# Two of the nine moves of an attention round issued by ScalarE instead of SyncE

## The reference

```
latent_kv = x @ w_kv_down ; kv = latent_kv @ w_kv_up ; k, v = split(kv)
q = x @ w_q
att = softmax(where(causal, q @ k.T * 64**-0.5, -inf))
y = (att @ v) @ w_out
```

## Time and profile before

| | |
|---|---|
| median of 3 runs | 1727.76 us (1726.07 to 1730.22) |
| the profiled execution | 1725.72 us, of which its span 1724.4 us |
| PE busy | 1661.7 us, 96% of the span |
| DVE busy | 1228.0 us, 71% |
| ACT busy | 848.3 us, 49% |
| POOL busy | 867.3 us, 50% |
| moves issued by SP | 864 (576 from prob, 288 from hx) |
| granted clock of PE | 0.997 of full speed |

### The profile page before, as it was taken

How to read it: one execution, slowest core, us unless ns; L and a number is a source line. 1 busy time by engine, 2 the same in 40 slices (tenths; PEclk the granted TensorE clock), 3 DMA queues, 4 the chain that set the end, 5 groups by cost and what they waited for, 6 DMA issues and landing times.

```text
span 1724.4 us, 41078 instructions
## 1 busy us (share of the span) xinstructions
PE 1661.7 (96%) x16518; PEld 1135.8 (66%) x16518; DVE 1228.0 (71%) x2678; ACT 848.3 (49%) x1864; POOL 867.3 (50%) x1123
## 2 busy tenths in 40 slices
PE   8999999999999999999999999999999999999997
PEld 5566685768566667566856667756684666766667
DVE  4988947727698994762679887675367999677445
ACT  5667624233576763422357765432245776433233
POOL 2788852231188884232128888314114888741410
PEclk9999999999999999999999999999999999999999
DMA  6566572231565655041346655405035666620504
GB/s 191 125 150 153 137 183 85 42 58 47 159 148 137 146 141 168 1 73 26 83 138 154 146 138 137 149 2 98 1 113 137 143 150 142 156 104 2 98 0 124
DMA packets 143853, 189.11 MB, mean 110 GB/s; under 512 B 34512, under 2 KB 107696, under 8 KB 142640
## 3 DMA queue, kind: packets, MB, share of 16 engines
q1 hardware_dynamic: 125472, 179.14, 42.4%
q10 hardware_dynamic: 18192, 7.35, 1.9%
HBM read 88.32 MB, written 13.16 MB: 59 GB/s over the span
## 4 chain that ended last, share of the span: by engine, by line
PE 66%; DVE 14%; ACT 5%; SPq 4%; POOL 4%; DMA 3%; issue 3%; ACTq 0%; POOLq 0%; DVEq 0%
PE scores L470 13%; PE bank L681 9%; PE scores L661 8%; PE bank L470 5%; DVE prob L800 4%; SPq L1011 4%; ACT prob L916 3%; DMA placed<-prob 3%; POOL placed L864 3%; PE scores L1718 2%; PE bank L718 2%; PE bank L708 2%; PE scores L441 2%; PE scores L1780 2%; PE bank L712 2%
## 5 line engine op out<-in xcount | busy, mean ns | idle before, releaser
L864 POOL COPY placed<-prob 32x768 f32<-32x768 f32 x448 | 368.3, 822 | 213.9 <-DVE prob L800 183.1
L301 POOL TENSOR_TENSOR rstd<-rstd,minus_half 128x2 f32<-128x2 f32 x96 | 69.9, 729 | 502.1 <-DVE rstd L300 500.0
L681 PEld LDWEIGHTS bank<-placed,v_t 128*64 128x64 f32 x4608 | 250.7, 137 | 75.7 <-issue 74.1
L681 PE MATMUL bank<-placed,v_t 128*64 128x128 f32 x4608 | 272.6, 274 | 11.8 <-DMA placed<-prob 9.0
L661 PE MATMUL scores<-k_t,q_t 64*128 64x512 f32 (+3 forms) x1536 | 274.0, 496 | 1.2 <-DVE neg_max L793 1.2
L800 DVE STREAM_TRANSPOSE prob<-prob 128x1536 f32<-128x1536 f32 x128 | 222.6, 1764 | 44.9 <-ACT prob L916 44.6
L793 DVE CUSTOM_DVE_ANT_0 mod_rows<-scores,hx 128x128 f32<-128x128 f32 (+7 forms) x256 | 190.7, 745 | 32.3 <-PE scores L661 32.3
L661 PEld LDWEIGHTS scores<-k_t,q_t 64*128 64x128 f32 x1536 | 130.1, 187 | 113.1 <-issue 92.2
L864 POOL COPY placed<-hx 32x768 f32<-32x768 f32 x224 | 184.3, 823 | 34.5 <-DVE hx L800 17.9
L916 ACT ACTIVATE prob<-mod_rows,neg_max 128x128 f32<-128x128 f32 (+2 forms) x192 | 137.7, 717 | 117.3 <-DVE neg_max L793 113.6
L793 DVE CUSTOM_DVE_ANT_0 x<-scores,hx 128x128 f32<-128x128 f32 (+7 forms) x256 | 192.7, 753 | 0.0
(11 more groups left out here) (256 smaller groups left out, 3139.0 us busy)
## 6 DMA issues: line engine op xcount, KB each, us to landing
placed<-prob SPq DMA_DIRECT2D x576, 96.0 KB, 2.5
f<-in_L_ffn_f SPq DMA_DIRECT2D x16, 2048.0 KB, 13.4
placed<-hx SPq DMA_DIRECT2D x288, 96.0 KB, 2.2
inverse_wide<-inverse_scratch SPq DMA_DIRECT2D x64, 256.0 KB, 4.2
slots_scratch<-high_rows SPq DMA_DIRECT2D x16, 512.0 KB, 6.3
inter<-slots_scratch SPq DMA_DIRECT2D x32, 256.0 KB, 4.8
mod_rows<-mod_scratch SPq DMA_DIRECT2D x32, 128.0 KB, 5.1
out<-x SPq DMA_DIRECT2D x16, 256.0 KB, 2.1
```

What stands on the lines that cost most here:

```text
L301: step = pool.do(lambda e, ts=ts: nc.gpsimd.tensor_tensor(rstd[:, ts], rstd[:, ts], minus_half[:, ts], op=ALU.pow), var, filled)
L681: last = nc.tensor.matmul(out_bank[rows_, at_:at_ + P], v_t[pair % 2][:, j, rows_], placed[m % 2][:, :, head, first_block(m, i) + j, :], s ...
L864: nc.gpsimd.tensor_copy(placed[m % 2][target * GROUP:(target + 1) * GROUP, source, :, :, :], prob[m % 3][source * GROUP:(source + 1) * GRO ...
```

## The change

The nine moves of a round are split. SP issues the first seven. The other two, (source 1, target 2) and (source 3, target 2), are issued by ACT, in a new function `last_moves`, behind the two exponentials of the first tile of the next round; in a round of type 0 this is in front of `store_inverse` (and, in round 3, of a projection's copy). The two of the stage's last round are issued behind ACT's last exponentials. Semaphores and counts stay the same: PE waits for all nine.

```diff
+        SP_MOVES, ACT_MOVES = MOVES[:7], MOVES[7:]
...
+            def last_moves(m):
+                e.wait_ge(flow["shuffled"], base["shuffled"] + HEADS * (m + 1))
+                if m > 1:
+                    e.wait_ge(flow["values_done"], base["values_done"] + m - 1)
+                for source, target in ACT_MOVES:
+                    e.dma_start(placed[m % 2][target * GROUP:(target + 1) * GROUP, source, :, :, :],
+                                prob[m % 3][source * GROUP:(source + 1) * GROUP, target, :, :, :]
+                                ).then_inc(flow[MOVED[m % 2]], 16)
...
                 for i in range(large):
                     for head in range(HEADS):
                         exponential(m, i, head)
+                    if i == 0 and m > 0:
+                        last_moves(m - 1)
                     if i == 0 and first_of_pair and m > 0:
                         if m == 3:
                             job(*jobs[0])
...
                 if first_of_pair:
                     next_weights(m)
+            last_moves(ROUNDS - 1)
             store_inverse(PAIRS - 1)
...
-                for source, target in MOVES:
+                for source, target in SP_MOVES:
```

## The result

| | before | changed |
|---|---|---|
| median | 1726.97 us (4 runs) | 1749.85 us (4 runs, 1745.74 to 1752.51) |
| ratio | | 1.0129, 95% interval 1.011 to 1.0148 |
| span of the profiled execution | 1724.4 us | 1746.9 us |

The change made the kernel slower by 1.3%, about 22 us. The sign and one of two mechanisms were forecast; the size is 1.7 times the forecast 13 us, at the very edge of the likeliest case's own range (1732 to 1750 us) and inside the full one.

What follows compares the result with a forecast made beforehand. PE, 96% busy, was taken as the bound; ACT's issues would make the DVE and ACT loop slower: 3 x 3.3 + 4.3 = 14.2 us, taken as 13, forecast 1741 us. Range 1726 to 1757, likeliest case 1732 to 1750.

Steps and rivals of the forecast that it cites:

- The gain on SP's side: SP's seven issues instead of nine: last move starts 1.27 us earlier; gain between nothing and PE's 10.6 us of waits.
- The price of an issue: One move issued on ACT: taken as 0.55 us, bounds 0.39 and 0.59 us; two with gaps 1.18 us.
- A: Rival: an ACT issue costs 0.39 us, PE sets the pace, the landing gain wins; 1719 us, chance 0.12.
- B: Rival: small issue price but landings don't move, or more slack in the loop; about 1728 us, chance 0.21.
- D: Rival: ACT and SP sequencers take turns issuing, two moves cost 2.3 us; about 1830 us, chance 0.03.
- Type 0, 1.15 us: Type 0 rounds: the moves in front of `store_inverse` delay ACT's next exponential from 576.46 to 577.6, cost 1.15 us.
- path M: Type 0's late transpose, SP's issues, last landing, PE's values; forecast for an isolated round: last move still 0.6 us earlier.
- The loop and its sum: DVE and ACT loop, per triple (a pair's three rounds): 22.98 + 1.35 = 24.33 us against PE's floor of 23.85.
- The check on the first triple: A stage's first triple, 22.98 us, taken to confirm the 23.0 us loop, so 0.87 us to spare.
- Cost 0.2 us: Type 2 rounds: issues end at 570.59, the large exponential started at 570.36; cost 0.2 us in the loop.
- rival C: ACT pays more than 0.59 us an issue, say 0.75; a triple takes 25.1 us; 1764 us, chance 0.10.
- The end of the stage: Behind round 21 POOL works without pause and PE waits for it, so the stage's lateness passes on one to one.

Runs made afterwards that it cites:

- both places mended: Changed kernel, ACT's two issues moved behind the third tile's exponentials in type 0 and behind the second large exponential in type 2: 1723.7 us, ratio 0.9975.
- only type 2 mended: Changed kernel, ACT's two issues moved behind the second large exponential in type 2, left behind the first tile in type 0: 1739.0 us, ratio 1.0064.
- type 0 alone: Changed kernel, but ACT issues moves in rounds of type 0 only; SP keeps all nine for the others: 1740.0 us, ratio 1.008.
- the one that only kept the engine busy for the same 1.2 us: Kernel before, no DMA moved, thirteen extra 128x1 exponentials on ACT behind the first tile's in type 0: 1737.5 us, ratio 1.0049.
- types 1 and 2: Changed kernel, but SP keeps all nine moves that fall in rounds of type 0: 1740.4 us, ratio 1.0077.
- type 2 alone: Changed kernel, but ACT issues moves in rounds of type 2 only: 1742.5 us, ratio 1.0081.
- type 2's place alone left bad: Changed kernel, ACT's issues put behind all tiles but the largest (type 0: third tile); types 1 and 2 unchanged: 1739.7 us, ratio 1.0074.

## Why the prediction was right, and where its size was off

- **The gain on SP's side.** Forecast: between nothing and 10.6 us. PE's waits for placed fell to 2.0 us, so the mechanism of the gain is real. In the change it is hidden by what follows; with both places mended (2.9 us of waits) the kernel is 0.25% faster, 4 of the 10.6 us.
- **The price of an issue.** Taken 0.55 us, measured 0.57 to 0.60 in the median. Rivals A, B and D of the prediction fall. The page "Perfetto Trace Analysis" of the Trainium skill (section "DMA Instruction — HWDGE (DVE, Sync)") has the wait for the shared descriptor generator inside the duration. A full turn of waiting isn't what this trace shows: beside SP's 0.59 us issues ACT's were no longer than that in the median.
- **Type 0, 1.15 us.** The third exponential is 1.3 us later against the first, since the second move costs 0.65 us and `store_inverse` 0.60 instead of 0.51. That this is a cost of its own is shown by the run with only type 2 mended (+11 us). The run with type 0 alone (+13 us) and the one that only kept the engine busy for the same 1.2 us (+9 us) show the cost of the delay too, but there SP still has nine moves, and it arrives through them (path M). The prediction had this path as an isolated round, "the last move still 0.6 us earlier"; in the change, with seven moves on SP, it was right not to count it.
- **The loop and its sum.** Forecast 24.33 us for a middle triple; batch 3 has (971.74 - 947.52) = 24.22 us, and a chain there without any PE link. But the number was right through two errors, by luck. DVE's idle time behind ACT grew by 1.2 (type 0, without the 0.43 us that PE caused), 0.23 (type 1, where I had put nothing) and 0.27 us (type 2, said 0.2): 1.7 instead of 1.35 us. And the loop without PE was about 0.4 us shorter than the 22.98 us that I gave it, as far as 24.24 - 1.7 tells (24.24 us is the mean of the five middle triples of batch 3); so it had more than 0.87 us to spare. The check on the first triple had misled me: 22.98 us is from the moves of round 0 to those of round 3. Counted from minimum to minimum, as the 24.49 us are, the first triple of batch 3 took 904.42 - 882.00 = 22.42 us, without the 0.37 us copy that the usual round of type 0 has.
- **What failed: "Cost 0.2 us" for type 2.** I counted it as a part of the loop, which had 0.87 us to spare. It also lies on path P, from scores over the large exponential and the copy to PE's projection of v, which had next to nothing to spare. In the kernel before, in round 14, the copy waited 0.19 us for the values and ended at 572.33; PE's second half of the projection followed at about 572.5:

```profile
571.68 0.65 ACT L924 COPY yT<-bank 128x384 f32<-128x384 f32 x2 [0.19 <-PE bank L681]
```

  The runs with types 1 and 2, or type 2 alone, put it at 13 to 14 us for the kernel, as large as the whole forecast. It and the loop don't add. Against the kernel before, the change is 22 us slower, type 2's place alone left bad 13, type 0's alone left bad 11, and both mended 4 us faster; in the mean of batch 3's middle triples, each place by itself already makes 24.2 us, and both together make 24.2 us as well.
- **Where the rest lies.** The middle triples of batches 2 and 4 are 24.4 to 26.1 us long. Some triples contain single long issues, as this one in round 2 of batch 3, whose first triple is 25.62 us:

```profile
906.88 0.52 ACTq L938 DMA_DIRECT2D placed<-prob  x1
...
907.43 1.87 ACTq L938 DMA_DIRECT2D placed<-prob  x1
...
909.35 1.04 ACT L917 ACTIVATE hx<-mod_rows,neg_max 128x896 f32<-128x896 f32 x1 [1.40 <-DVE neg_max L794]
```

Before, SP had such issues too (1.96 us at most), where ACT's exponentials didn't stand behind them. This was rival C in part: the tail, not the median. In the changed kernel the 184 issues of moves on ACT that the timeline lists singly exceed 0.62 us by 8.4 us in sum, so the tail can't make more than about that of the remaining 9 us (22 less the forecast 13); how much it makes, and what holds such an issue up, stays open. The triple of 26.06 us, in batch 4 from 1350.34 us on, has another part: from 1354.8 to 1358.6 us PE's granted clock was 0.55, most of it at the lower level (1.2 GHz). PE had stood still for 2.10 us just before, waiting for ACT's copy, and 16 instructions of scores then took 3.89 us instead of 2.86. The kernel before has such stretches too (0.66 from 762 to 767 us), so its clock wasn't quite at the upper level "in all stretches"; there, they lie outside the pair stages.

- **The end of the stage** passed the lateness on, as forecast: 22.3 us in the four stages, 22.5 us in the span. It is one to one in the sum; behind a single stage up to 2 us were lost or regained.

## What to carry to other kernels

An engine that is busy for half of the time isn't free to issue DMAs: its stream stands still for each issue, and that costs nothing only where the engine already holds work, or waits anyway, for as long as all issues in that place take. So choose the place by what is queued there, and then follow each instruction behind it to whoever waits for it, the copies that empty a bank for PE as well as the next link of the loop; the slack of one path says nothing about another. And read the chain of each experiment, not only its time: two runs here had the time that one theory forecast and got it on another path. With the same two moves on ACT the kernel was 1.3% slower when they stood behind the first tile, and 0.25% faster when they stood further down, in type 0 two tiles later, in type 2 behind the second large exponential.

## What the runs showed of the hardware that I had not expected

Of two moves issued in a row on ACT, the first mostly took 0.51 to 0.54 us and the second mostly 0.60 to 0.87 us; a store behind them took 0.59 us in the median instead of 0.53. SP, which issues its nine in a row, shows the same step without any move on ACT: in the chain of the run with thirteen small exponentials its first issue of a round took 0.54 us and the next ones 0.59 and 0.60. So the step comes with the place in a row of issues, and not, or not only, with the other engine's issues. ACT can issue a DMA while instructions that precede it in program order are still executing or queued on its engine: at 1011.38 the first move is issued although the second exponential starts only at 1011.58. Six 128x1 exponentials of 0.19 us delayed the next instruction by 0.56 us, half of their sum.
